# Attention values kept with heads on partitions: turns of values replaced by transfers, in a fused attention and expert kernel

## The reference

```python
qkv = (x @ w_qkv).reshape(b, s, 3, N_HEADS, HEAD_DIM)
scores = jnp.einsum('bqhd,bkhd->bhqk', q, k) * SCALE
attn = jax.nn.softmax(scores, axis=-1)
out = jnp.einsum('bhqk,bkhd->bqhd', attn, v).reshape(b, s, d) @ w_proj + b_proj
x = _layernorm(x + out)
x = _layernorm(x + experts(x))     # top_k of x @ Wg.T, gelu(h) * gate, W1, W2
```

## Time and profile before

| what | value |
|---|---|
| median of 3 runs | 3198.0 us (3197.28 to 3198.33) |
| the profiled execution's own time | 3197.97 us |
| its span, first to last instruction | 3196.2 us |
| busy in the span: PE, DVE, ACT, POOL | 2954.4, 2440.1, 2209.5, 1771.9 us |

### The profile page before, as it was taken

How to read it: one execution, slowest core, us unless ns; L and a number is a source line. 1 busy time by engine, 2 the same in 40 slices (tenths; PEclk the granted TensorE clock), 3 DMA queues, 4 the chain that set the end, 5 groups by cost and what they waited for, 6 DMA issues and landing times. The chain is left out here.

```text
span 3196.2 us, 63612 instructions
## 1 busy us (share of the span) xinstructions
PE 2954.4 (92%) x21037; PEld 1919.7 (60%) x21037; DVE 2440.1 (76%) x5277; ACT 2209.5 (69%) x4282; POOL 1771.9 (55%) x2036
## 2 busy tenths in 40 slices
PE   7999999979999999999999979999999999999940
PEld 4454544534444544445454438888888888888840
DVE  7888888868887888888888757767766677676758
ACT  3888888868887888888888765666665566566620
POOL 4567677657676776767767444333433433433343
PEclk8999999989999999999999999999999999999975
DMA  3555555433333333333333347878877877778759
GB/s 117 157 165 173 173 166 175 126 88 100 83 108 85 96 100 85 106 90 98 100 82 106 82 111 143 177 150 168 164 152 149 162 161 164 157 157 162 154 139 315
DMA packets 412530, 435.23 MB, mean 136 GB/s; under 512 B 223017, under 2 KB 313521, under 8 KB 412209
## 3 DMA queue, kind: packets, MB, share of 16 engines
q1 hardware_dynamic: 356144, 346.36, 43.8%
q0 software_dynamic: 51168, 67.68, 10.2%
q10 hardware_dynamic: 4896, 17.17, 1.4%
HBM read 183.93 MB, written 146.15 MB: 103 GB/s over the span
## 5 line engine op out<-in xcount | busy, mean ns | idle before, releaser
L1650 DVE TENSOR_REDUCE peak<-ps 128x1 f32<-128x512 f32 x2048 | 1321.8, 682 | 295.9 <-PE ps L996 290.3
L1168 ACT ACTIVATE probs<-ps 128x512 f32<-128x512 f32 x2048 | 1109.4, 619 | 187.0 <-PE ps L1006 179.0
L1006 PE MATMUL ps<-stack 50*128 50x512 f32 x2048 | 727.2, 440 | 5.6 <-DVE peak L1650 2.2
L996 PE MATMUL ps<-stack 48*128 48x512 f32 x2048 | 719.9, 437 | 6.3 <-DVE peak L1650 3.0
L996 PEld LDWEIGHTS ps<-stack 48*128 48x128 f32 x2048 | 335.4, 188 | 421.7 <-issue 255.6
L1024 PE MATMUL ps<-probs,v 128*17 128x512 f32 x4096 | 542.3, 601 | 1.1 <-ACT probs L1168 1.1
L668 POOL DMA_INDIRECT x<-o,out_token x144 | 231.2, 1605 | 370.4 <-ACT o L1077 331.1
L1470 DVE TENSOR_TENSOR v<-ps,v 128x512 f32<-128x512 f32 (+1 forms) x288 | 187.8, 656 | 305.8 <-ACT v L1063 305.3
L949 PE MATMUL ps<-w_buf,qk_hi 128*128 128x256 f32 x2160 | 386.9, 281 | 1.9 <-DVE qk_lo L1475 1.9
L668 POOL DMA_INDIRECT x<-y,out_token x126 | 201.7, 1601 | 324.6 <-ACT y L1077 196.5
L935 PE MATMUL ps<-x_t_hi,stack 128*128 128x512 f32 x1152 | 364.7, 398 | 9.0 <-DVE v L1470 7.0
(11 more groups left out here) (222 smaller groups left out, 5200.2 us busy)
## 6 DMA issues: line engine op xcount, KB each, us to landing
stack<-qk_hi SPq DMA_DIRECT2D x1020, 64.0 KB, 2.3
expert_rows<-blank SPq DMA_DIRECT2D x81, 520.0 KB, 4.1
xs<-in_L_ffn_W SPq DMA_DIRECT2D x144, 256.0 KB, 4.5
probs<-in_L_ffn_W SPq DMA_DIRECT2D x144, 256.0 KB, 4.4
probs<-in_L_ffn_W SPq DMA_DIRECT2D x72, 512.0 KB, 5.9
stack<-qk_lo SPq DMA_DIRECT2D x510, 64.0 KB, 2.3
qk<-expert_rows SPq DMA_DIRECT2D x168, 128.0 KB, 6.1
xs<-in_L_attn_x SPq DMA_DIRECT2D x32, 512.0 KB, 4.2
```

The lines of the kernel that those rows point to most:

```text
L996: pe.matmul(ps[it.bank(("rows", n))][:], q_stack[s][part, h, t * P:(t + 1) * P], k_stack[s][part, h, :], start=True, stop=True).then_inc(s ...
L1006: pe.matmul(ps[it.bank(("cols", n))][:], k_stack[g][part, h, t * P:(t + 1) * P], q_stack[g][part, h, :], start=True, stop=True).then_inc(s ...
L1168: act.activation(probs[:, j % RING, :], ps[it.bank(("cols", s * UNITS + j))][:], ACT.Exp, scale=SCALE).then_inc(s_exp, 1)
L1650: dve.tensor_reduce(peak[s % 2][:, u:u + 1], ps[it.bank(("rows", n))][:], AX.X, ALU.max, negate=True).then_inc(s_max, 1)
```

## The change

The values are no longer turned. After each group's last pv step SP sends `pv` to memory and fetches it back so that the channels of all heads stand in order on the partitions of `o_t` (`values_out`, `values_in`). The four rows of sums go by a transfer to 32 partitions of 64 elements each (`sums`); DVE takes the reciprocals of two groups at once (`inverses`, after units 14 and 41), and two transfers bring them back, repeated on the 16 partitions of each head (`inverse_out`, `inverse_in`). POOL then multiplies half of `o_t` at once (`normalise(0)`, `normalise(1)`). The rounds `turn0` to `turn3` and `oT` are gone. The scatter of a sequence is moved an iteration later, in four parts. The table ORDER, the queues of SP and POOL and the places of DVE's routing and statistics are written anew; the last blank rows are written an iteration earlier; in the last two iterations POOL, ACT and DVE have their own order. The expert part stores one of its two output tiles in the memory of `o_t`.

Of the table ORDER these two lines show the form:

```diff
-    ["place", 0, 1, "oT", "pv", 2, 3],
+    [0, 1, "pv", 2, 3, "qk3"],
```

The core of the rest:

```diff
+TURNED = (14, 41)
+LEADS = (2, 4)
...
+def values_of(s):
+    return cols_of(s - 1) if s else (1, -1)
...
-        out = [o, y]
+        out = [o_t[:].rearrange("p k n -> p (k n)").rearrange("p (t c) -> p t c", c=DIM), y]
...
+                def values_out(s):
+                    g, off = values_of(s)
+                    if it.on(off):
+                        n, k, a = (b + off) * GROUPS + g, g // 2, g % 2
+                        sp.wait_ge(s_pvout, n + 1)
+                        wait(sp, s_inverse, (b + off) * KT + (k - 1))
+                        sp.dma_start(sums[k][32 * a:32 * a + 32],
+                                     pv[HD:P:32].rearrange("h (j n) -> h j n", j=SLICES)).then_inc(s_sums[k], 16)
+                        wait(sp, s_o_rows[k], 16 * (2 * (b + off) + a - 1))
+                        sp.dma_start(pv_dram[g], pv[:]).then_inc(s_pv_rows, 16)
+                def values_in(s):
+                    g, off = values_of(s)
+                    if it.on(off):
+                        n, k, a = (b + off) * GROUPS + g, g // 2, g % 2
+                        sp.wait_ge(s_pv_rows, 16 * (n + 1))
+                        if b + off > 0:
+                            sp.wait_ge(s_full, it.full("proj1", off))
+                        sp.dma_start(o_t[HALF * a:HALF * (a + 1), k],
+                                     pv_dram[g].rearrange("(h r) n -> h r n", r=32)[:, 0:HD]).then_inc(s_o_rows[k], 16)
+                def inverse_out(k):
+                    if it.on(-1):
+                        n = (b - 1) * KT + k
+                        sp.wait_ge(s_inverse, n + 1)
+                        wait(sp, s_inverse_in, 16 * n)
+                        sp.dma_start(inv_dram[k].rearrange("h (j n) -> (h j) n", j=SLICES),
+                                     inverse[k][:]).then_inc(s_inverse_out, 16)
+                def inverse_in(k):
+                    if it.on(-1):
+                        n = (b - 1) * KT + k
+                        sp.wait_ge(s_inverse_out, 16 * (n + 1))
+                        wait(sp, s_o, n)
+                        heads = inv_dram[k].rearrange("(h a) n -> h a n", a=1)
+                        sp.dma_start(inverse_rows[:], heads.to_broadcast([P // HD, HD, SEQ])).then_inc(s_inverse_in, 16)
...
+                        if half_ == 0:
+                            wait(sp, s_cols, (b + (off - 1)) * 64 + (UNITS * (g + 1)))
+                            settle(sp, s_waited_sp)
+                            sp.wait_ge(s_lo, 2 * (g // 2) + 2 if first_seq else (b + off) * 4 + 4)
...
+                def fill(s):
                     if it.filling:
-
-
-                        if it.known:
-                            sp.wait_ge(s_blank, 2)
+                        sp.wait_ge(s_blank, 2)
                         for e in (2 * s, 2 * s + 1):
                             sp.dma_start(table_rows[b + e * per],
                                          blank[:].rearrange("p t c -> p (t c)")).then_inc(s_fill, 16)
-                    if s == 3 and it.known and b == per:
-                        sp.dma_start(table_rows[EXPERTS * per], blank[:].rearrange("p t c -> p (t c)")).then_inc(s_fill, 16)
+                        if s == 3 and b == per - 1:
+                            sp.dma_start(table_rows[EXPERTS * per],
+                                         blank[:].rearrange("p t c -> p (t c)")).then_inc(s_fill, 16)
...
+                if it.last():
+                    first_units()
+                stacks(0, 0)
+                stacks(0, 1)
+                fill(0)
+                values_out(0)
+                peaks(0)
+                inverse_out(0)
+                store_rows()
+                inverse_in(0)
+                load_x()
+                stacks(1, 0)
+                values_out(1)
+                peaks(1)
+                values_in(0)
+                stacks(1, 1)
+                values_in(1)
+                fill(1)
+                stacks(2, 0)
+                values_out(2)
+                stacks(2, 1)
+                inverse_out(1)
+                peaks(2)
+                values_in(2)
+                inverse_in(1)
+                peaks(3)
+                stacks(3, 0)
+                values_out(3)
+                stacks(3, 1)
+                fill(3)
+                values_in(3)
+                fill(2)
...
+                def normalise(k):
+                    if it.on(-1):
+                        pool.wait_ge(s_o_rows[k], 32 * b)
+                        pool.wait_ge(s_inverse_in, 16 * ((b - 1) * KT + (k + 1)))
+                        pool.tensor_tensor(o_t[:, k, :], o_t[:, k, :], inverse_rows[:], ALU.mult).then_inc(s_o, 1)
...
+                def scatter(part, ago=3):
+                    q = b - ago
+                    if 0 <= q < n_seq:
+                        if part == 0:
+                            pool.wait_ge(s_token, q + 1)
+                            pool.wait_ge(s_fill, (q + 1) * (16 * EXPERTS) if q + 2 < per else FILLED)
+                            settle(pool, s_waited_pool)
+                        for c in (2 * part, 2 * part + 1):
+                            pool.indirect_dma_start(
+                                table, bass.IndirectOffsetOnAxis(ap=slot[:, c:c + 1], axis=0),
+                                row[q % 2][:, c % TILES, :], None,
+                                bounds_check=EXPERTS * cap - 1, oob_is_err=False).then_inc(s_scatter, 16)
...
+                split_x()
+                scatter(0)
+                split_qk(0)
+                split_qk(1)
+                split_qk(2)
+                count_experts()
+                scatter(1)
+                scatter(2)
+                scatter(3)
+                normalise(0)
+                find_slots()
                 normalise(1)
-                if it.on(1) and b >= 0:
-                    split_qk(0)
-                    split_qk(1)
-                if it.on(-2):
-                    count_experts()
-                normalise(2)
...
                     if n == 0:
-                        result_of("oT")
+                        pe.wait_ge(s_o, (b - 1) * KT + KT)
...
-                    g, off = cols_of(s - 1) if s else (1, -1)
+                    g, off = values_of(s)
                     if it.on(off):
-                        act.wait_ge(s_pv, (b + off) * 16 + (4 * g + 4))
-                        before_ = {0: ("turn0", -1), 1: ("turn1", 0), 2: ("turn2", 0), 3: ("turn3", 0)}[s]
-                        if (b + off) * 4 + g > 0:
-                            act.wait_ge(s_full, it.full(*before_))
+                        n = (b + off) * GROUPS + g
+                        act.wait_ge(s_pv, 4 * n + 4)
...
+                def inverses(k):
+                    if it.on(-1):
+                        dve.wait_ge(s_sums[k], 32 * b)
+                        wait(dve, s_inverse_out, 16 * ((b - 1) * KT + (k - 1)))
+                        dve.reciprocal(inverse[k][:], sums[k][:]).then_inc(s_inverse, 1)
...
-                        if which == 11 and it.on(-1 if where < 3 else 0):
-                            turn(f"turn{(where + 1) % 4}", (where + 1) % 4)
+                        if UNITS * where + which in TURNED:
+                            inverses(TURNED.index(UNITS * where + which))
```

236 lines of the change are left out of this document (113 added, 123 removed).

## The result

The changed kernel takes 3486.44 us (median of 4 runs, 3481.64 to 3492.53), the kernel before beside it 3198.16 us: a ratio of 1.0899, 95% interval 1.0875 to 1.0923. It is slower by 288 us; the forecast was 3204 us, and 3255 us at the most. The profiled execution took 3490.79 us, its span 3488.9.

The account below looks back on a forecast made before the run. PE bounds the kernel before (56.5 us an iteration), SP's in-order queue the changed one (57.0). 3198 less 29 one-off, plus 10.5 (21 iterations) and 25 (10 with fills), gave 3204 us; range 3125 to 3255.

Parts of the forecast that it names:

- leg 1: From unit 0 to unit 32, along SP's queue: the pieces for unit 32 are there at 27.5 us.
- The places of the waits, units 32 and 0: PE would wait there for `q_stack` and `k_stack` transfers, 1 and 1.5 to 2 us.
- The 18 us wait: PE's one-off 18.25 us wait, caused by the last blank rows, goes; with the half clock after it, 19.0 us.
- the third rival: PE's clock falls at the waits at units 32 and 0: 1.2 us each time, at most 3.4; middle 3260 us; chance 0.10.
- The landing of the pieces for unit 32: End of the first leg: the last piece starts at 24.8 us and lands after 2.3, at 27.1; 0.4 added for slowing.
- `inverse_in`: Second leg's 256 KB load: starts at 10.5 us, lands after 3.0, before `find_slots` ends; at 4.0 it is 0.35 late.
- Leg 2: From unit 32 to the next unit 0: DVE 12.1, POOL 6.8, SP's issues and landing 10.6, together 29.5 us.
- PE and DVE alone: An iteration set by PE's and DVE's work in the new order: 54.8 us, the middle of 52.4 to 57.2.
- Fills: Iterations 0 to 9, SP's queue between units 0 and 16: blank rows add 2.0 us; slower rival 3234 to 3254, chance 0.13.
- PE's pace: Faster rival: SP's two legs fall under 54.8 us and PE sets the iteration; 3126 us, chance 0.31.

Follow-up runs that it names:

- mend: The kernel before, with only the last blank rows written one iteration earlier: 3181.3 us, ratio 0.9935 to the kernel before.
- spread: The changed kernel, with the dimension of 16 outermost in the loads of values and of reciprocals (the latter now two loads): 3363.0 us.
- short_v: The changed kernel, with loads of values fetching 64 of 512 columns from the second sequence on: 3353.8 us.
- short_i: The changed kernel, with loads of reciprocals writing 64 of 512 columns from the second sequence on: 3410.4 us.
- order_only: The changed kernel, with all transfers of values, sums and reciprocals left out from the second sequence on: 3285.0 us, ratio 1.0253.
- order_even: order_only with the round `qk2` moved from c5 to the empty c7 and `v1` from c13 to the empty c14: 3299.8 us.
- spread_pool: spread with the last split of q and k ahead of POOL's second multiplication of `o_t`: 3421.6 us.
- spread_act: spread with the sums and `pv` sent to memory by ACT instead of SP: 3370.5 us.
- spread_all: spread with the split ahead of POOL's second multiplication, blank rows issued by ACT, and `peak0` and `peak2` one unit later on PE: 3548.4 us.
- order_peak: order_only with the rounds `peak0` and `peak2` one unit later in PE's order: 3293.1 us.
- mend_later: mend with PE's rounds `x1T` and `qk0` one unit later each: 3179.4 us, ratio 0.9934 to the kernel before.

## Why the prediction was wrong

**What went as worked.** The first half of leg 1 is exact: SP issues the reciprocals at 11.4 us (forecast 11.3), they land after 2.0, `inverse_in` starts at 13.44 (13.3). From `route_over` to the end of the split POOL needs 6.5 us without its wait (6.8). The places of the waits, units 32 and 0, are the ones named. The 18 us wait went, and mend puts its worth at 20.6 us (19.0). The clock fell, as the third rival said.

**The landing of the pieces for unit 32 (the step that failed).** "The last of the six following pieces ... lands after 2.3, at 27.1" took the landing of a piece with no large load ahead of it on its engines. It took 4.84 us in this iteration, 5.1 at the median, because a load of values ahead of it (6.6 us at the median) held 4 of the 16 engines. With the issues, which took 12.8 us from `inverse_in` to the last piece instead of 11.5 (slowing 1.3 instead of 0.4), leg 1 is 31.1 us, not 27.5. spread and short_v show the cause: in both the last piece lands after 2.25 us again. The prediction gave the loads of values their issues and no landing time; what they do to the pieces behind them was a term put at nothing, but for 0.4 us each at the upper bound.

**`inverse_in`.** I took 3.0 us, with 4.0 as the bound, from transfers that run on all engines. (The Trainium skill, DMA: Bandwidth & Descriptors, "Anatomy of one DMA", has 2.0 us and the bytes, an estimate of 2.6; the section gives this for transfers that POOL issues, and this one is SP's. The trace does not agree.) It lands after 4.7 us at the median and 5.15 here, on 8 engines. It also starts at 13.3 us of the second leg instead of 10.5: SP waited 3.8 us for ACT's copy of `pv`, which was late because unit 32 was, and the prediction has no such wait. Since `find_slots` ended 2.3 later too, neither delay alone would have held POOL up here; together they give its wait of 2.17. With an eighth of its bytes (short_i) 76 us go, over a third of the transfers' loss: the term that I let change nothing in the sum.

**Leg 2.** 34.5 us, not 29.5: `route_over` is done at 14.3 instead of 12.1, as DVE waits 2.4 us in all for PE there, 1.4 of it while PE works at the half clock; 2.2 for the reciprocals; 0.7 in SP's issues. The two legs, 31.1 and 34.5, are the 65.6 us of the iteration: the frame was right, its prices were not.

**PE and DVE alone, 54.8 us (52.4 to 57.2).** order_only measures 57.4 at full clock, above the bound, and 58.8 with the clock. The middle of a range was chosen where the bound was nearer. What I didn't see are the places where POOL's long operations hold DVE's small ones (`peak2`, and the routing in c6), and that the maxima's rounds stand where DVE is latest. Whether the 2.4 us in c7 and its like come from these places alone stays open: order_even shows that they are not cured by moving rounds.

**The clock.** The rival was priced at 1.2 to 3.4 us an iteration and given 0.10. It cost 5.2 (175.7 less 15.1, over 31). Of the 34 falls in iterations 11 to 29, 25 come behind a gap of 1.1 to 3.7 us, and nine as in iteration 15, behind the gaps in c4 and c7 and ahead of the wait at unit 32, which the prediction did not look for. What decides is not shown: with the same two gaps the clock stays at 1.00 in iterations 12 and 13 of order_only and falls in others. A slower PE also makes DVE's results, and with them SP's, later again. The rival's own arithmetic was off besides: the middle of 3204 + 37 to 105 is 3275, not 3260.

**Fills.** 2.0 us over an iteration without them were forecast, 4.6 measured (69.4 less 64.85). In iteration 5 `sums` was issued at 12.6 (11.5) and took 3.9 us to land (2.0), and DVE waited. The place was right, the mechanism in part: order_only, which sends no sums after the first sequence, still pays 5.0, and what PE waits for at unit 16 in both kernels are the pieces of maxima behind the blanks, which the prediction names, without a price of their own.

**Chances.** The cases were put beside each other, as if only one could happen; landing, clock and fills came together, which the range, up to one of them alone, did not hold. The case that was given 0.31, PE's pace, needed an earlier DVE and quicker issues; neither came.

## What to carry to other kernels

Before a transfer is given a landing time, look at the outermost dimension of both its sides: 4 heads outside meant 4 of 16 engines, 6.6 us instead of 2.8 for 128 KB, and the pieces behind it late. A profile tells it by the semaphore's steps, and a missing landing time is a reason to count them; putting the dimension of 16 outside took 123 us off. And in a program whose queues wait in order, an edit that removes one wait (spread_pool, spread_act, spread_all, order_peak) mostly shows where the next one stands; follow what is behind it on each queue before pricing the gain.

## What the runs showed of the hardware that was not expected

- Transfers with 4 or 8 rows outermost ran on 4 or 8 DMA engines: 128 KB in 6.6 us, 256 KB in 4.7; the same 128 KB on 16 engines in 2.8. 64 KB pieces queued behind one took 5.1 us instead of 2.3.
- A DVE operation on 128x16 elements took 1.11 us instead of 0.17 beside a POOL multiplication of two inputs, and ended 0.03 us after it; inside POOL's scaling of rows (TENSOR_SCALAR, 1.22 us) such operations in order_only took 0.21 us at most.
- The clock fell after gaps of 0.65 and 0.57 us 9 us apart, with PE busy between; in iterations 12 and 13 of order_only the same two gaps left it at 1.00. Filling two of the gaps with matmuls brought it from 0.92 to 0.97.
- 8 KB issued behind two blanks of 520 KB on one queue took 3.9 us to land; with the blanks on ACT's queue the same transfer, in the same iteration, took 1.8.
- One chip ran the kernel before in 3429 us instead of 3200, at a granted clock of 0.93 instead of 0.97. In mend_later's trace from it the waits between engines are longer, while maxima and exponentials take their usual time. Its ratios did not agree with those of other chips.
